# A fused block on Trainium2: differential attention that normalises and adds each unit as it comes, and a modulated weight made beside the gate scan

## The chip, the cores and the metric

The kernel runs on one core of a Trainium2 chip. The metric is the device time of one execution in microseconds (us). The engines are TensorE (PE for its matmuls, PEld for its weight loads), VectorE (DVE), ScalarE (ACT), GpSimd (POOL) and SyncE (SP), which issues DMAs. Each runs its own queue of instructions in order; they wait for each other through semaphores (`wait_ge`, `then_inc`).

## The reference, cut to what matters

The reference is a chain of eight stages over x of 8 batches x 256 tokens x 128 features, with a condition vector per batch. The change touches the last four; the first four (two attentions, a GRU-like scan with a top-1 mixture of experts, its routing) stay as they are.

```
# 1. gate scan: a recurrence over the 256 tokens, per batch, started from cond
g    = sigmoid(W_s s + W_x x_t + b)
s    = tanh(g * x_t + (1 - alpha) * s)
# 2. differential attention on the scan's states
q1,q2 = s @ w_q12 ; k1,k2 = s @ w_k12 ; v = s @ w_v
A    = softmax(q1 k1^T * scale) - lambda * softmax(q2 k2^T * scale)
o    = (1 - 0.8) * rmsnorm(A v)            # over the 128 features, eps 1e-5
x    = x + o
# 3. modulated linear map, per batch b
m    = (x * y_b) @ W / sqrt(sum((W*y_b)^2) + 1e-8)      # y_b = cond_b / sqrt(128)
# 4. top-2 mixture of 8 experts on m (silu gated, 512 wide), gate scores m @ gate^T
out  = x + sum over the two experts of p_e * expert_e(m)
```

(The listing is shortened by hand to the computation that the kernel carries out; q and k are 128 wide, 2,048 tokens in all.)

## The kernel before

`program` calls one function per stage; each opens a block in which every engine gets its list of instructions, and the engines meet between blocks. Features lie on the 128 partitions in `xT`, with the column of token t of batch b at 8 t + b.

**`gate_scan`** (block at L1555) runs 256 steps. In a step TensorE multiplies the state with `wT` (L1595), ScalarE takes the sigmoid (L1635), VectorE scans `targ` (L1676), ScalarE takes tanh (L1638) and VectorE scales the state by `leak` (L1673). TensorE fills the wait with 14 matmuls nobody reads (L1625). Work for later stages is dealt over the steps: every tenth step turns an expert weight (L1607, kept by ScalarE at L1645), and `plan` puts "qk" items (one matmul group, L1616) and "v" items (two strided blocks of states as stationary operands, L1621) on other steps, each with 4 fillers in place of 14 and copied by ScalarE one step later (L1656). `plan` avoids the steps of the weights.

**`diff_attention`** (block at L1723) first makes lambda (L1738, L1806), the modulation's sum (L1741), the last 32 tokens of q and k (L1749, copied at L1814) and the second half of the values (L1753, copied at L1817). Then 16 units, u = 2 b + half, each 128 queries against 256 keys of batch b. For unit u TensorE makes two score maps (`scores`, L1762), VectorE their maxima (`maxima`, L1874, L1876), ScalarE two exponentials with sums (`exps`, L1825), VectorE the reciprocals and the difference (`difference`, L1881 to L1889), TensorE turns it (`turn`, L1771), ScalarE keeps it (L1833), TensorE multiplies with the values (`attend`, L1780), VectorE copies the head (L1894) and ScalarE sums its squares (L1844). The orders are written out by hand: TensorE goes scores(u+2), attend(u-1), turn(u); VectorE maxima(u+1), difference(u), keep(u-1); ScalarE exps(u+1), keep(u), square(u-1). Two buffers each. After all units come one Sqrt (L1851), a reciprocal (L1905), 16 scalings (L1910), 16 transposes (L1800) and four additions into `xT` (L1915).

**`sparse_experts`** (block at L1991) first scales xT by `ys` (L2153), multiplies with `wmod` (L2009), scales by `dr` into `mB` (L2160), makes the gate scores (L2013) and copies them (L2178). Then the router: `best` twice (L2167 to L2175), counting, positions, lists. Beside it TensorE and ScalarE turn m and x to token-major `mt` and `xt` (L2004, L2089) and SP stores m to DRAM (`mrow`, L2334). POOL gathers blocks of 128 rows of `mrow` (L2312) once the lists are there, and 39 blocks go through the experts (L2049, L2058, L2066), are scattered to `yrow` (L2317), read back and added to `xt` (L2290).

Of the kernel before, what the change touches and what calls it, by code (L numbers as in the profile page):

```python
# [33 lines left out]
P = 128  # L34
# [27 lines left out]
def allocate(nc, ctx):  # L62
# [22 lines left out]
    n.ys, n.dr = sb("ys", [P, B]), sb("dr", [P, B])  # L85
# [6 lines left out]
    n.load_experts = ctx.enter_context(nc.semaphore("load_experts"))  # L92
    n.load_linear = ctx.enter_context(nc.semaphore("load_linear"))
# [1406 lines left out]
def gate_scan(nc, n, a, s2, qk, vt, wgT, wuT, wdT):  # L1500
# [13 lines left out]
    SPAN = 32  # L1514


    plan, at = {}, 0
    for p in range(T // SPAN - 1):
        at = max(at, SPAN * (p + 1))
        for item in [("qk", p, k) for k in range(4)] + ([("v", p, k) for k in range(4)] if SPAN * (p + 1) == P else []):  # L1520
            at += 1
            while (at - 4) % EVERY in (0, 1) or at % G == INPUTS_AT:
                at += 1
            plan[at] = (len(plan),) + item
    assert at < T
    with ExitStack() as local:
# [7 lines left out]
        leak = sb("leak", [P, 1])  # L1534
        ones_w = sb("ones_w", [1, B * G])
# [14 lines left out]
        arg_done = sem("s_arg"); state = sem("s_state")  # L1550

# [3 lines left out]
        with nc.Block() as block:  # L1555
# [12 lines left out]
            def _(pool):  # L1568
                for q in range(4):
                    w = TOK // 4  # L1570
                    out = pairs[:, 2 * w * q:2 * w * (q + 1)].rearrange("p (x two) -> p two x", two=2)[:, 0]
                    pool.tensor_copy(out, n.xT[:, w * q:w * q + w]).then_inc(z_in, 1)

            @block.tensor
            def _(pe):
# [16 lines left out]
                for s in range(T):  # L1592
# [16 lines left out]
                    if s in plan:  # L1609
# [3 lines left out]
                        if kind == "qk":  # L1613
# [3 lines left out]
                                                  s2[:, c0:c0 + B * SPAN], start=True, stop=True)  # L1617
                        else:
# [9 lines left out]
            def _(act):  # L1628
# [4 lines left out]
                for s in range(T):  # L1633
# [12 lines left out]
                    if s - 1 in plan:  # L1646
# [3 lines left out]
                        if kind == "qk":  # L1650
# [5 lines left out]
                        nc.scalar.activation(out, src, ACT.Copy).then_inc(pj_kept, 1)  # L1656
# [23 lines left out]
def diff_attention(nc, n, s2, qk, vt):  # L1680

    SPAN = 32
    MOD_EPS = 1e-8
# [3 lines left out]
    UNITS = B * SEG  # L1690
    with ExitStack() as local:
# [3 lines left out]
        def ps(name, shape):  # L1695
            return local.enter_context(nc.psum_tensor(name, shape, F32))
# [5 lines left out]
        negmax = [sb(f"negmax{i}", [P, 2]) for i in range(2)]  # L1702
        sums = [sb(f"sums{i}", [P, 2]) for i in range(2)]
        inv = [sb(f"inv{i}", [P, 2]) for i in range(2)]
# [3 lines left out]
        heads = sb("heads", [P, UNITS, D])  # L1708
        junk = sb("d_junk", [P, D])
        squares = sb("squares", [P, UNITS])  # L1710
        ys2, w2, dsum, mod_eps = sb("ys2", [P, B]), sb("w2", [P, D]), sb("dsum", [P, B]), sb("m_eps", [P, 1])
# [11 lines left out]
        with nc.Block() as block:  # L1723
# [10 lines left out]
            def _(pe):  # L1734
# [53 lines left out]
                for u in range(UNITS + 1):  # L1788
                    if u + 2 < UNITS:
                        scores(u + 2)  # L1790
                    if u >= 1:
                        attend(u - 1)
# [607 lines left out]
```

## Time and profile before

| what | value |
|---|---|
| runs before: median, lowest, highest | 1583.0, 1581.71, 1587.13 us |
| profiled execution: its time | 1581.07 us |
| its span, first to last instruction | 1579.0 us |
| TensorE matmul, VectorE, ScalarE, POOL busy | 93%, 46%, 41%, 7% of the span |
| mean granted TensorE clock | 0.946 of full (2.4 GHz) |

The span is what the trace covers; the execution's time has some 2 us around it. Busy shares are means over stages with different limits, and much of TensorE's share is filler, so the stages have to be read one by one. A line of a timeline gives the start in us from the span's start, the duration, the engine, the line of the kernel, the operation, output and input tiles, their shapes and how many instructions were merged. In brackets stands the idle time before it and who ended it.

### The profile page before, as it was taken

What the parts mean: (1) busy time and instruction counts of PE and PEld (TensorE: products, weight loads), DVE (VectorE), ACT (ScalarE), POOL (GpSimd) and SP (SyncE); (2) the same over time, 40 slices, a digit from 0 to 9 for tenths busy, and PEclk for the clock granted to TensorE, in tenths of its full rate; (3) what the DMA queues carried; (4) which work ended last, traced back from release to release, by engine and by line L of the source; (5) the groups of instructions that cost most, each with busy time, mean ns of one, the idle gap of its engine ahead of it and who ended that gap; (6) DMA issues with size and microseconds to landing.
All of it is one profiled execution on the core that took longest, in us unless ns stands there. A gap on an engine that the chain in (4) does not pass through costs nothing. (4 is left out here: it accounts for less than half of the span.)

```text
span 1579.0 us, 30235 instructions
## 1 busy us (share of the span) xinstructions
PE 1460.8 (93%) x11078; PEld 1132.5 (72%) x11078; DVE 732.8 (46%) x2721; ACT 651.0 (41%) x2429; POOL 106.7 (7%) x141
## 2 busy tenths in 40 slices
PE   7999978999989999999999998799999999767995
PEld 5333324777779999999999996488888888644663
DVE  3576765455433444444444445633333332863223
ACT  2322204565524554554554552134444443622442
POOL 4000000000000000000000000100000000004662
PEclk8999989999999999999999998599999999957998
DMA  5000000000030000000000000100000000001113
GB/s 158 1 0 0 1 0 1 1 1 1 1 108 1 1 2 2 1 2 1 2 1 2 1 2 1 34 21 22 22 22 28 22 2 1 1 27 33 42 43 96
DMA packets 27724, 27.95 MB, mean 18 GB/s; under 512 B 2293, under 2 KB 22234, under 8 KB 27450
## 3 DMA queue, kind: packets, MB, share of 16 engines
q1 hardware_dynamic: 20970, 16.70, 3.6%
q0 software_dynamic: 2496, 5.12, 1.1%
q10 hardware_dynamic: 4112, 4.19, 0.9%
q8 instruction: 90, 1.47, 0.4%
q14 instruction: 56, 0.46, 0.1%
HBM read 21.35 MB, written 4.65 MB: 16 GB/s over the span
## 5 line engine op out<-in xcount | busy, mean ns | idle before, releaser
L1625 PE MATMUL spare<-identb 128*128 128x128 bf16 x3166 | 218.4, 219 | 0.0
L1625 PEld LDWEIGHTS spare<-identb 128*128 128x128 bf16 x3166 | 202.0, 103 | 4.3
L1223 DVE TENSOR_TENSOR_SCAN narg<-rz,pre_n 128x16 f32<-128x16 f32 x256 | 47.9, 187 | 220.2 <-PE pre_n L1120 219.0
L1158 ACT ACTIVATE ghid<-gh_ps,cols 128x128 f32<-128x128 f32 x512 | 144.3, 365 | 12.9 <-PE gh_ps L1059 12.7
L1059 PE MATMUL gh_ps<-hist,w 128*128 128x128 f32 x1024 | 137.5, 275 | 0.6 <-ACT ghid L1158 0.6
L1068 PE MATMUL gy_ps<-w2e,ghid 128*128 128x128 f32 x1024 | 136.8, 276 | 0.8 <-DVE g_diff L1204 0.3
L1068 PEld LDWEIGHTS gy_ps<-w2e,ghid 128*128 128x128 f32 x1024 | 124.4, 191 | 3.2 <-issue 3.2
L1059 PEld LDWEIGHTS gh_ps<-hist,w 128*128 128x128 f32 x1024 | 125.9, 188 | 0.8 <-DVE hist L1231 0.8
L1144 ACT ACTIVATE rz<-pre_r 128x8 f32<-128x8 f32 x256 | 45.6, 178 | 181.9 <-PE pre_r L1120 179.2
L1120 PE MATMUL pre_r<-hist,gru_w 128*128 128x128 f32 x512 | 118.1, 311 | 0.8 <-DVE hist L1231 0.5
L1676 DVE TENSOR_TENSOR_SCAN targ<-gates,pairs 128x16 f32<-128x16 f32 x256 | 49.1, 192 | 140.8 <-ACT gates L1635 140.8
L1595 PEld LDWEIGHTS s_pre<-s,wT 128*128 128x128 f32 x512 | 77.0, 190 | 40.6 <-ACT s L1638 40.0
L1120 PE MATMUL pre_z<-hist,gru_w 128*128 128x128 f32 x512 | 99.9, 276 | 0.0
L1595 PE MATMUL s_pre<-s,wT 128*128 128x8 f32 x512 | 98.0, 264 | 2.0 <-ACT s L1638 0.4
L1120 PE MATMUL pre_n<-hist,gru_w 128*128 128x128 f32 x512 | 99.7, 276 | 0.0
L1673 DVE TENSOR_SCALAR pairs<-s,leak 128x8 f32<-128x8 f32 x256 | 59.6, 233 | 70.6 <-ACT s L1638 70.5
L1635 ACT ACTIVATE gates<-s_pre 128x8 f32<-128x8 f32 x256 | 45.5, 178 | 108.1 <-PE s_pre L1595 108.1
L634 DVE TENSOR_TENSOR term<-bc,kb 128x512 f32<-128x512 f32 x96 | 64.9, 686 | 53.3 <-PE bc L382 53.2
L1120 PEld LDWEIGHTS pre_r<-hist,gru_w 128*128 128x128 f32 x512 | 77.1, 190 | 16.0 <-DVE hist L1231 1.3
L1638 ACT ACTIVATE s<-targ 128x8 f32<-128x8 f32 x256 | 53.4, 209 | 83.9 <-DVE targ L1676 83.9
L1120 PEld LDWEIGHTS pre_n<-hist,gru_w 128*128 128x128 f32 x512 | 77.6, 189 | 0.0
L1120 PEld LDWEIGHTS pre_z<-hist,gru_w 128*128 128x128 f32 x512 | 77.5, 189 | 0.0
(412 smaller groups left out, 2516.4 us busy)
## 6 DMA issues: line engine op xcount, KB each, us to landing
w<-in_L_ffn_W SPq DMA_DIRECT2D x1, 2048.0 KB, 9.6
raw<-in_L_ffn_wg SPq DMA_DIRECT2D x8, 256.0 KB, 3.0
raw<-in_L_ffn_wu SPq DMA_DIRECT2D x8, 256.0 KB, 2.8
raw<-in_L_ffn_wd SPq DMA_DIRECT2D x8, 256.0 KB, 2.7
wqkv<-in_L_attn_Wqkv SPq DMA_DIRECT2D x1, 1536.0 KB, 6.6
mrow<-mt SPq DMA_DIRECT2D x4, 256.0 KB, 2.4
y_top<-yrow SPq DMA_DIRECT2D x4, 256.0 KB, 5.4
y_next<-yrow ACTq DMA_DIRECT2D x4, 256.0 KB, 5.8
```

The lines of the kernel that those rows point to most:

```text
L634: nc.vector.tensor_tensor(term[u % 2][:, j, :].rearrange("p (b t) -> p b t", b=GB), bc[k % 2][:, :].rearrange("p (b t) -> p b t", b=GB), k ...
L1059: mm = nc.tensor.matmul(h_ps[:, f, :], w1[:, e, P * f:P * f + P], tokens(g), start=True, stop=True)
L1068: mm = nc.tensor.matmul(y_ps, hid[v % 2][:, f, :], w2[:, e, f, :], start=(f == 0), stop=(f == NF - 1))
L1120: nc.tensor.matmul(out, n.gru_w[:, i, :], h, start=False, stop=True, skip_group_check=True).then_inc(ready, 1)
L1144: nc.scalar.activation(second(rz[s % 2][:, 0:16]), gate_slot(pre_r, s), ACT.Sigmoid).then_inc(r_done, 1)
L1158: nc.scalar.activation(hid[v % 2][:, f, :], h_ps[:, f, :], ACT.Relu, bias=n.cols[:, at:at + 1]).then_inc(h_done, 1)
L1223: V.tensor_tensor_scan(narg[p][:, :], rz[p][:, 0:16], n_slot(s), 0.0, ALU.mult, ALU.add).then_inc(narg_done, 1)
L1595: nc.tensor.matmul(pre[s // G % 2][:, at:at + B], wT[:, 0, :], s2[:, 8 * s:8 * s + B], start=False, stop=True, skip_group_check=True).then ...
L1625: nc.tensor.matmul(spare[:, 0:P], n.identb[:, :], n.identb[:, :], start=True, stop=True)
L1638: nc.scalar.activation(s2[:, 8 * s + 8:8 * s + 16], second(targ[s % 2][:, :]), ACT.Tanh).then_inc(state, 1)
L1673: nc.vector.tensor_scalar(second(pair), s2[:, 8 * s:8 * s + 8], leak[:, 0:1], None, ALU.mult).then_inc(leaked, 1)
L1676: nc.vector.tensor_tensor_scan(targ[s % 2][:, :], gates[s % 2][:, :], pair, 0.0, ALU.mult, ALU.add).then_inc(arg_done, 1)
```

## The change

The diff does five things.

1. `diff_attention` normalises each unit by itself. GpSimd computes `unit = (squares + least)^(-1/2)`, where `least` carries the epsilon and is scaled by the square of the first softmax's sum, since the difference is no longer divided by it: `difference` makes `ratio = sum0 * lambda / sum1` and one pass `probs1 * ratio + probs0`. ScalarE squares straight from PSUM with scale 1/GAIN.
2. The residual is token-major: `norm` adds `o * unit` into `xt[:, u, :]`. `xt` is filled in the gate scan by 8 "x" items (two transposes of strided columns of `xT` each).
3. Per batch a modulated weight `wb[:, b, :]` (128 columns of `W` scaled, then 8 gate columns) is made in the gate scan: one "mod" item, GpSimd's power and eight scalings (`wrow`), and 8 "w" items. In `diff_attention`, after the two norms of a batch, `turn_x(b)` transposes the new x, `keep_x(b)` copies it, `modulate(b)` multiplies with `wb`, `keep_m(b)` copies m and the gate scores into `mt`, and SP stores m per batch.
4. q is stored negated and scaled, so that VectorE takes minima and no scaling follows. The entry is reordered: q and k first, lambda behind them, values inside the units (`values(0)` behind `scores(0)`, `values(1)` to `values(3)` at the end of iterations 3, 7 and 11). ScalarE's Exp table is loaded ahead.
5. The front of `sparse_experts` up to the copy of the scores, and all its turning of m and x, are gone; it begins with `best` on `mt`.

```diff
 # gate_scan
+    put(4, [("x", 0, b) for b in range(B)])
+    put(20, [("mod", 0, 0)])
+    for p in range(T // SPAN - 1):
+        put(SPAN * (p + 1), [("qk", p, k) for k in range(4)])
+        if p == 0:
+            put(at, [("w", 0, b) for b in range(B)])
...
+                    if q == 0:
+                        pool.memset(power[:, :], -0.5).then_inc(mod_ready, 1)
+                        pool.tensor_scalar(ys[:, :], n.condT, float(D) ** -0.5, None, ALU.mult).then_inc(mod_ready, 1)
+                        pool.tensor_tensor(w2[:, :], n.wmod[:, :], n.wmod[:, :], ALU.mult).then_inc(mod_ready, 1)
+                        pool.wait_ge(mod_ready, 3)
+                        pool.tensor_tensor(ys2[:, :], ys[:, :], ys[:, :], ALU.mult).then_inc(mod_ready, 1)
+                pool.wait_ge(pj_kept, mod_item + 1)
+                pool.tensor_scalar(dr[:, :], modT[:, D:D + B], MOD_EPS, None, ALU.add).then_inc(dr_done, 1)
+                pool.wait_ge(dr_done, 1)
+                pool.tensor_tensor(dr[:, :], dr[:, :], power[:, :], ALU.pow).then_inc(dr_done, 1)
+                pool.wait_ge(dr_done, 2)
+                for b in range(B):
+                    pool.tensor_scalar(wrow[:, b, :], modT[:, 0:D], dr[:, b:b + 1], None, ALU.mult).then_inc(wrow_done, 1)
...
+                        elif kind == "x":
+                            for j in range(2):
+                                tokens = n.xT[:, :].rearrange("p (t b) -> p b t", b=B)[:, k, P * j:P * j + P]
+                                mm = nc.tensor.transpose(pj[i % 2][:, P * j:P * j + P], tokens, n.ident[:, :])
+                        elif kind == "mod":
+                            pe.wait_ge(mod_ready, 4)
+                            nc.tensor.transpose(pj[i % 2][:, 0:D], n.wmod[:, :], n.ident[:, :])
+                            mm = nc.tensor.matmul(pj[i % 2][:, D:D + B], w2[:, :], ys2[:, :], start=True, stop=True)
+                        elif kind == "w":
+                            pe.wait_ge(wrow_done, k + 1)
+                            g0 = ROWS["gate"][0]
+                            nc.tensor.transpose(pj[i % 2][:, 0:D], wrow[:, k, :], n.ident[:, :])
+                            mm = nc.tensor.matmul(pj[i % 2][:, D:D + E], wrow[:, k, :], n.cols[:, g0:g0 + E], start=True, stop=True)
 # diff_attention, GpSimd
+                for u in range(UNITS):
+                    one = slice(u, u + 1)
+                    pool.wait_ge(exp_done, 2 * u + 1)
+                    pool.tensor_scalar(least[:, one], sums[:, u, 0:1], D * EPS / GAIN ** 2, None, ALU.mult).then_inc(least_done, 1)
+                    pool.wait_ge(least_done, 2 * u + 1)
+                    pool.tensor_tensor(least[:, one], least[:, one], sums[:, u, 0:1], ALU.mult).then_inc(least_done, 1)
+                    pool.wait_ge(least_done, 2 * u + 2)
+                    pool.wait_ge(sq_done, u + 1)
+                    pool.tensor_tensor(mean[:, one], squares[:, one], least[:, one], ALU.add).then_inc(mean_done, 1)
+                    pool.wait_ge(mean_done, u + 1)
+                    pool.tensor_tensor(unit[:, one], mean[:, one], power[:, :], ALU.pow).then_inc(unit_done, 1)
 # TensorE
+                def turn_x(b):
+                    pe.wait_ge(normed, 2 * b + 2)
+                    pe.wait_ge(x_kept, turns["x", b])
+                    for i in range(SEG):
+                        mm = nc.tensor.transpose(x_ps[:, P * i:P * i + P], xt[:, SEG * b + i, :], n.ident[:, :])
+                    mm.then_inc(x_in, 1)
+
+                def modulate(b):
+                    pe.wait_ge(x_kept, turns["x", b] + 1)
+                    if b:
+                        pe.wait_ge(m_kept, b)
+                    for i in range(SEG):
+                        mm = nc.tensor.matmul(m_ps[:, M * i:M * i + M], xf[b % 2][:, i, :], wb[:, b, :], start=True, stop=True)
+                    mm.then_inc(m_in, 1)
...
+                for u in range(LAST + 1):
                     if u + 2 < UNITS:
                         scores(u + 2)
+                    if u >= 5 and u % 2:
+                        modulate((u - 5) // 2)
+                    if 1 <= u <= UNITS:
                         attend(u - 1)
                     if u < UNITS:
                         turn(u)
+                    if u in (3, 7, 11):
+                        values((u + 1) // 4)
+                    if u >= 4 and u % 2 == 0:
+                        turn_x((u - 4) // 2)
 # VectorE
+                    V.reciprocal(inv1[p][:, :], sums[:, u, 1:2]).then_inc(inv_done, 1)
...
+                    V.scalar_tensor_tensor(ratio[p][:, :], sums[:, u, 0:1], lam[:, 0:1], inv1[p][:, :],
+                                           ALU.mult, ALU.mult).then_inc(ratio_done, 1)
...
+                    V.scalar_tensor_tensor(diff[p][:, :], probs[p][:, 1, :], ratio[p][:, 0:1], probs[p][:, 0, :],
                                            ALU.mult, ALU.add).then_inc(diff_done, 1)
...
+                def norm(u):
+                    dve.wait_ge(unit_done, u + 1)
+                    V.scalar_tensor_tensor(xt[:, u, :], o_ps[u % 2], unit[:, u:u + 1], xt[:, u, :],
+                                           ALU.mult, ALU.add).then_inc(normed, 1)
...
+                minima(0)
+                keep_values(0)
+                for u in range(LAST + 1):
                     if u + 1 < UNITS:
+                        minima(u + 1)
+                    if u < UNITS:
+                        difference(u)
+                    if 2 <= u < UNITS + 2:
+                        norm(u - 2)
+                    if u in (3, 7, 11):
+                        keep_values((u + 1) // 4)
+                    if u >= 4 and u % 2 == 0:
+                        keep_x((u - 4) // 2)
+                    if u >= 5 and u % 2:
+                        keep_m((u - 5) // 2)
+            @block.sync
+            def _(sp):
+                for b in range(B):
+                    sp.wait_ge(m_kept, b + 1)
+                    sp.dma_start(mrow[T * b:T * b + T, :].rearrange("(i p) d -> p i d", p=P),
+                                 mt[:, SEG * b:SEG * b + SEG, 0:D]).then_inc(n.m_stored, 16)
 # sparse_experts, POOL
-                pool.wait_ge(m_stored, 16 * 4)
+                pool.wait_ge(n.m_stored, 16 * B)
```

## Rows read from the trace of the kernel before

**Rows 1.** Table of stretches: busy us and instructions per engine, clock, DMA
```profile
1332.70:1344.70 12.00, 10.38 (x35) 8.80 (x36) 0.68 (x5) 5.09 (x11) 0.99 (x4) 0.73 0.00 0
1344.70:1381.50 36.80, 28.25 (x150) 22.28 (x150) 32.40 (x110) 24.69 (x107) 0.00 (x0) 0.95 0.00 1
1381.50:1408.40 26.90, 18.04 (x67) 12.63 (x66) 15.04 (x34) 2.86 (x8) 1.81 (x10) 0.58 0.00 1
```

**Rows 2.** Timeline of the gate scan: a step with v, then one with qk
```profile
1185.32 1.19 PE L1621 MATMUL s_pj<-wv,s 128*128 128x128 f32 x4
...
1187.22 0.19 DVE L1676 TENSOR_TENSOR_SCAN targ<-gates,pairs 128x16 f32<-128x16 f32 x1 [0.75 <-ACT gates L1635]
...
1256.42 0.19 DVE L1676 TENSOR_TENSOR_SCAN targ<-gates,pairs 128x16 f32<-128x16 f32 x1 [0.49 <-ACT gates L1635]
...
1257.61 0.19 DVE L1676 TENSOR_TENSOR_SCAN targ<-gates,pairs 128x16 f32<-128x16 f32 x1 [0.49 <-ACT gates L1635]
```

**Rows 3.** Timeline of the attention's entry
```profile
1332.94 1.28 ACT L1806 ACT_TABLE_LOAD   x1 [0.31 <-PEq L1555]
...
1334.38 1.60 PE L1749 MATMUL dpj<-s,wq 128*128 128x256 f32 x4
...
1336.01 1.05 ACT L1814 ACTIVATE qk<-dpj 128x256 f32<-128x256 f32 x2 [1.28 <-PE dpj L1749]
...
1342.54 3.78 PE L1762 MATMUL s_ps<-qk 128*128 128x256 f32 x8 [0.47 <-ACT vt L1817]
1344.72 0.69 DVE L1874 TENSOR_REDUCE negmax<-s_ps 128x2 f32<-128x512 f32 x1 [9.93 <-PE s_ps L1762]
```

**Rows 4.** Timeline of one unit in the middle
```profile
1350.94 0.68 DVE L1874 TENSOR_REDUCE negmax<-s_ps 128x2 f32<-128x512 f32 x1
...
1351.74 0.16 DVE L1881 RECIPROCAL inv<-sums 128x2 f32<-128x2 f32 x1
...
1352.20 0.35 DVE L1887 TENSOR_SCALAR diff<-probs,inv 128x256 f32<-128x256 f32 x1
...
1352.59 0.48 DVE L1889 SCALAR_TENSOR_TENSOR diff<-probs,inv,diff 128x256 f32<-128x256 f32 x1
...
1352.99 0.28 DVE L1894 COPY heads<-o_ps 128x128 f32<-128x128 f32 x1
...
1353.13 0.44 PE L1771 MATMUL dt_ps<-ident,diff 128*128 128x128 f32 x2 [0.50 <-DVE diff L1889]
1353.19 0.68 DVE L1874 TENSOR_REDUCE negmax<-s_ps 128x2 f32<-128x512 f32 x1
...
1353.60 0.38 ACT L1833 ACTIVATE diffT<-dt_ps 128x256 f32<-128x256 f32 x1 [0.66 <-PE dt_ps L1771]
1353.88 0.30 ACT L1844 ACTIVATE d_junk<-heads 128x128 f32<-128x128 f32 x1
```

**Rows 5.** Timeline from the last difference to the router's first reduction
```profile
1380.96 0.48 DVE L1889 SCALAR_TENSOR_TENSOR diff<-probs,inv,diff 128x256 f32<-128x256 f32 x1
...
1382.41 1.04 PE L1780 MATMUL o_ps<-vt,diffT 128*128 128x128 f32 x4 [0.47 <-ACT diffT L1833]
...
1394.02 2.59 DVE L2153 TENSOR_TENSOR xs<-xT,ys 128x512 f32<-128x512 f32 x4 [0.32 <-PEq L1723]
...
1408.42 0.29 DVE L2167 TENSOR_REDUCE m_v<-m_val 128x16 f32<-128x128 f32 x1
```

**Rows 6.** POOL's groups by shape (busy us, mean ns), and one issue of SP
```profile
L260 POOL TENSOR_SCALAR_AFFINE_SELECT pick<-pick 96x1024 bf16<-96x1024 bf16 x9 | 11.7, 1305 | 1.3
L1731 POOL TENSOR_TENSOR ys<-ys 128x8 f32<-128x8 f32 x1 | 0.2, 202 | 0.0
...
1183.34 0.34 SPq L1565 DMA_DIRECT2D raw<-in_L_ffn_wd  x1
```

**Rows 7.** First expert matmuls, and the stretch before the clock came back
```profile
1433.78 2.07 PE L2049 MATMUL gu<-wgT,xgT 128*128 x2 [0.49 <-DVE xgT L2271]
...
1403.20:1437.20 34.00, 19.69 (x96) 14.97 (x96) 19.61 (x54) 9.41 (x13) 6.59 (x7) 0.50 0.16 43
```

More of the change, by code:

```diff
@@ L1514, in gate_scan, with put @@
     SPAN = 32
+    SCALE = float(D) ** -0.25
+    MOD_EPS = 1e-8
     plan, at = {}, 0
-    for p in range(T // SPAN - 1):
-        at = max(at, SPAN * (p + 1))
-        for item in [("qk", p, k) for k in range(4)] + ([("v", p, k) for k in range(4)] if SPAN * (p + 1) == P else []):
+    def put(earliest, items):
+        nonlocal at
+        at = max(at, earliest)
+        for item in items:
             at += 1
@@ L1550, in gate_scan @@
         arg_done = sem("s_arg"); state = sem("s_state")
+        mod_ready = sem("mod_ready"); dr_done = sem("dr_done"); wrow_done = sem("wrow_done")
+        mod_item = next(item[0] for item in plan.values() if item[1] == "mod")
         def second(ap):
@@ L1707, in diff_attention @@
         diffT = [sb(f"diffT{i}", [P, SEG, P]) for i in range(2)]
[L1708 to L1711, printed above, removed]
-        rms = sb("rms", [P, UNITS]); unit = sb("unit", [P, UNITS]); eps = sb("d_eps", [P, 1])
-        pj = [ps(f"dpj{i}", [P, 512]) for i in range(2)]
-        s_ps = [ps(f"s_ps{i}", [P, 2, T]) for i in range(2)]
@@ L1721, in diff_attention @@
-        rms_done = sem("d_rms"); mod_ready = sem("mod_ready"); mod_in = sem("mod_in"); mod_kept = sem("mod_kept"); unit_done = sem("d_unit"); normed = sem("d_normed"); back_in = sem("d_back"); added = sem("d_added")
+        junk = [sb(f"d_junk{i}", [P, D]) for i in range(2)]
+        squares, least, mean = sb("squares", [P, UNITS]), sb("least", [P, UNITS]), sb("d_mean", [P, UNITS])
+        power, unit = sb("d_power", [P, 1]), sb("unit", [P, UNITS])
+        xf = [sb(f"xf{i}", [P, SEG, P]) for i in range(2)]
@@ L1723, in diff_attention @@
+        turns = {key: i for i, (key, _) in enumerate(sorted(turns.items(), key=lambda kv: kv[1]))}
         with nc.Block() as block:
@@ L1896, in _ @@
-                maxima(0)
-                for u in range(UNITS):
-                    if u + 1 < UNITS:
-                        maxima(u + 1)
-                    difference(u)
-                    if u >= 1:
-                        keep(u - 1)
-                keep(UNITS - 1)
-                dve.wait_ge(rms_done, 1)
-                V.reciprocal(unit[:, :], rms[:, :]).then_inc(link, 1)
-                dve.wait_ge(mod_kept, 2)
-                V.reciprocal(n.dr[:, :], dsum[:, :])
-                dve.wait_ge(link, UNITS + 1)
@@ L2020, in _ @@
                 nc.tensor.matmul(cum_ps, tri[:, :], taken[:, :, :], start=True, stop=True).then_inc(counted, 1)
-                for g in range(4, 8):
-                    turn_tokens(g)
                 pe.wait_ge(pay_done, 2)
@@ L2095, in _ @@
                 act.preload_act_table(ACT.Silu)
-                for g in range(4, 8):
-                    keep_tokens(g)
                 act.wait_ge(const, 2)
```

290 lines of the change are left out of this document (122 added, 168 removed).

## The prediction, made before the changed kernel was seen

> **What bounds the kernel now.** I read the table of stretches first [rows 1]. The change touches four places: the gate scan (1011.5 to 1332.7 us), the entry of the differential attention up to the first `maxima` (12.0 us), its sixteen units (36.8 us), and what lies between the last unit and the router's first reduction (26.9 us). In the entry VectorE is busy for 0.7 us of 12; in the units it is busy 32.4 us of 36.8, more than TensorE (28.3) and ScalarE (24.7); in the last stretch no engine is full and TensorE is granted 0.58 of its clock. So entry and tail are chains of waits, and the units are bound by VectorE.
>
> The timeline of the scan [rows 2] shows that a step lasts 1.19 us from one `targ` to the next, also in a step with a "qk" item (1256.42 to 1257.61), but in one with a "v" item, whose four loads of strided states hold TensorE 1.19 us, VectorE waits 0.75 us for the gates and not 0.49: the step is 0.26 longer. In the entry [rows 3] TensorE does lambda, the modulation sum, four matmuls for q and k and eight for values; `scores(0)` starts at 1342.54 and VectorE's first reduction at 1344.72. In one unit [rows 4] VectorE's starts follow each other without a gap; reduction to reduction is 2.25 us, and the last difference starts at 1380.96 [rows 5], so it is the sixteenth after 36.2 us. In the tail [rows 5] the last heads are squared, a Sqrt table is loaded, sixteen scalings, sixteen transposes, four additions into xT, the scaling by ys, four wide matmuls and 32 small ones at the low clock follow each other, until the router reduces at 1408.42. From there to the end of the span are 170.6 us that the diff leaves in order.
>
> **Gate scan.** Added: 17 items (8 "x", 1 "mod", 8 "w"), none on the steps that turn expert weights. An x item loads two strided blocks and w loads three that are not strided, where the v item loads four strided ones; beside them ten fillers fall away, as in a qk item. An x item should hold TensorE about half of the v item's 1.19 us, and ScalarE's copies are no wider than qk's. The cover is the filler time of the step; without it each item costs up to 0.26, as v does: 17 x 0.26 = 4.4 us. POOL's work (a sum of small operations and eight 128x128 scalings) runs beside about four steps. I take +0.3 us for all this; bounds 0 and 4.4. POOL's first power is also here, twelve steps before a w item wants it, so a slow first one is covered.
>
> **Entry.** Removed from the path: the wait for lambda and the modulation sum ahead of q and k, and the values, of which `values(0)` now stands behind `scores(0)` and the others inside the units. TensorE can start at about 1332.95. ScalarE loads its table until 1334.22 and copies q and k in four parts, 1.05 us for two [rows 3]: done at 1334.24 + 2.1 = 1336.35. q's four matmuls took 1.60 us where the stretch's clock was 0.73, so both are ready by 1336.2 at that rate and near 1334.6 at twice it. Then `scores(0)`: before, 2.18 us passed from its start to the reduction, at the low clock; at the full one half of it. First reduction: 1336.4 + 1.6 = 1338.0 (bounds 1337.3 and 1339.5) against 1344.72, a gain of 6.7 us (5.2 to 7.4). Lambda's exponential now comes behind the copies, at 1336.5, and is in time.
>
> **The units.** From VectorE's unit go the scaling of the maximum, one wide pass (`tensor_scalar` over 256) and the copy of the head; in come the norm (like the copy, 0.20 to the next start), and per unit from the fifth on one of `keep_x` and `keep_m` (a copy of 256 or 272 columns, about 0.35 to the next start from the 128-column copy's 0.20). Let d be the start of the difference's last pass. From the reduction's start to it: 0.62 (reduction to an independent follower; 0.80 less the scaling) + 0.46 (reciprocal to the pass after next [rows 4]) = about 1.05. Behind it 0.40 to the norm and 0.20 to what follows. Without keeps a step is 1.65, with one 2.0, against 2.25. But `keep_x(b)` waits for `turn_x(b)`, which stands in TensorE's order behind `turn(u)`, and this for this very difference: turn starts at d + 0.53 and ends at d + 0.98 [rows 4], two more transposes end at d + 1.22, so the copy starts at d + 1.26 instead of d + 0.62. VectorE, the bound engine, stalls 0.64 us in each even unit, and behind the waiting copy stand the next reduction and with it ScalarE's next exponentials: step 2.64. The odd ones are 2.01, because `modulate(b)` ran ahead of turn. The mean is 2.33, slightly over 2.25. In units 3, 7 and 11 `keep_values` waits for four strided loads behind turn (1.0 us more than the turn): d + 2.0, so steps of 3.4, 3.75 and 3.75.
> A second chain floors the step. The unit's turn (d + 0.98), ScalarE's copy (0.28 to the next start) and square with its accumulator (0.4), then POOL's addition and power, and the norm comes at the next d + 0.40: step at least 1.3 + 0.3 of waits + power = 1.6 + x. POOL's nearest row is 0.20 us for 128x8 [rows 6]; the dearest compute row with a repeated cost is 1.3 us (96x1024). I take x = 0.3, nearest the small tile; bounds 0.1 and 1.3.
> Steps between the sixteen differences: 1.45, 1.45, 2.05, 3.4, then (2.64, 2.01, 2.64, 3.75) twice, 2.64, 2.01, and 2.02 (no reduction in the last): 37.1. The first difference comes 2.95 after the first reduction, since `values(0)` pushes `scores(1)` back 1.0 us. 40.1 against 36.2: +3.8, and +0.7 for the first scores at the low clock: +4.5 us (bounds +2 and +6, without the power).
>
> The Trainium skill (SBUF — State Buffer, section Who interferes with whom) says that a VectorE instruction with two SBUF inputs and a GpSimd instruction that reads SBUF exclude each other for their whole length; the difference's last pass (0.48 us) is such a one. No row of the trace shows POOL and VectorE together in this stage. By the rule POOL's pair would be pushed behind that pass in the even units only, where the norm's delay of some 0.4 us hides in the wait for `turn_x`; the sum would change by two or three of the early steps, +1 us.
>
> **Tail.** From the end of the last difference (E = 1381.44) the new chain is: turn E + 0.49, ScalarE's copy 0.90, attend 1.6 (1.04 at the fallen clock [rows 5]), square 2.1, POOL 2.1 to 2.65, norm 2.95, turn_x 3.6, keep_x 4.0, modulate 4.9, keep_m 5.3, SP's issue of the last store 0.34 [rows 6], the change of block 0.32 [rows 5], the small ramp 0.25: E + 6.2 (bounds 5.6 and 7.5). Before: 1408.42 - 1381.44 = 27.0. Gain 20.8 us. The store itself is far ahead of the gathers, which wait for the lists 20 us later.
> Behind it the order is the same. But the first expert matmuls already ran at half clock for 3.5 us (1433.78 to 1437.2 [rows 7]), and TensorE now does less ahead of them: +0.8 us, between 0 (as now) and 2.
>
> **Sum.** +0.3 - 6.7 + 4.5 - 20.8 + 0.8 = -21.9. The profiled execution took 1581.07 us, its span and 2.1 around it: 1559.2. The median of the runs is 1.9 above it, so against that 1561.1; I forecast 1560.0.
>
> **Rivals.**
> The power is dear but bounded (1.3 us as POOL's large row): all steps under 2.9 grow to 2.9, 14 steps sum to 7.2 more, and the tail 1.0: 1568. For it: no row shows a power, and it should be no cheaper than an addition; against: it is one column, not 1,024.
> The other side: POOL's chain becomes the bound. From x = 2.4 us the fourteen steps of 1.6 + x (and x in the tail) eat all 21.9 us; at 3.0 us the time is 1591. For it: the trace has no row of its kind; against: 2.4 us is twelve times POOL's small tile [rows 6].
> The items in the scan don't fit: each costs as v does: 1564.
> The turns don't stall VectorE (its own steps 1.65 and 2.0, the values hidden): twelve steps of 2.0, four of some 1.7 and a first one of 2.0, 33 us instead of 40: 1553. Against: the order written for TensorE puts each turn behind `turn(u)`.
>
> **Chances.** The forecast 0.62 (its own range 1556 to 1566); dear power 0.15; slow items 0.10; no stalls 0.09; POOL the bound 0.04. Range of 8 in 10: 1552 to 1570. This kernel's measurement can't tell under 0.3% (4.7 us): only POOL's bound, or one near it, ends there: faster 0.94, same 0.03, slower 0.03.
>
> **What would show it.** Reductions that start near 1338; difference starts apart by 2.6 and 2.0 in turn with `xf` copies waiting for TensorE in the even units; scan steps of 1.19 with x and w items; the power's row at 0.3; some 6 us from the last difference to the router's first reduction. A POOL row of microseconds for the power, or `norm` waiting in every unit, would make it wrong.

## The result, and the profile of the changed kernel

The changed kernel took 1563.9 us (median of 4 runs, 1560.8 to 1565.1) beside 1582.4 us for the kernel before (4 runs, 1575.4 to 1587.1); the ratio of the runs is 0.989, with a 95% interval from 0.986 to 0.993. The forecast was 1560.0 us in a range of 1552 to 1570. The profiled executions span 1579.0 and 1563.3 us, 15.7 us apart. Of a kernel further down (E6) one execution of four took 3400.8 us, which nothing on record explains; it is left out of that kernel's ratio.

The two traces, cut at the same instructions (a stretch runs from the start of one to the start of the next):

| stretch, us | before | after | change | predicted |
|---|---|---|---|---|
| start to the first `targ` (no line on its way changed) | 1017.30 | 1019.54 | +2.24 | 0 |
| gate scan, to the last `targ` | 314.90 | 317.60 | +2.70 | +0.3 |
| entry, to the first reduction | 12.52 | 5.23 | -7.29 | -6.7 |
| units, to the start of the last difference | 36.24 | 41.20 | +4.96 | +4.5 |
| tail, to the router's first reduction | 27.46 | 8.53 | -18.93 | -20.8 |
| router, to the first `gu` weight load | 25.25 | 25.35 | +0.10 | 0 |
| experts, to the end | 145.33 | 145.89 | +0.56 | +0.8 |

The first line is no effect of the change: over twelve profiled executions, one of each kernel in this document and all with the same stages up to there, that stretch took between 1015.6 and 1023.2 us, so the time of a single profile can't settle 5 us. It is left out from here on. Behind it the change took away 17.9 us. A stretch in which the clock does the same can be read to tenths; the scan and the tail can't, where the clock falls at another place, and the scan of the eight kernels that have it as changed took 316.5 to 320.6 us.

The table of stretches, in the columns of [rows 1]: scan, entry, units, tail, and the stretch in which the clock is low.

```profile
1019.50:1337.10 317.60, 310.54 (x3736) 264.70 (x3735) 108.43 (x510) 130.82 (x607) 6.62 (x10) 0.98 0.06 18
1337.14:1342.37 5.23, 4.02 (x27) 3.51 (x25) 0.87 (x5) 3.40 (x7) 0.10 (x1) 1.00 0.00 0
1342.37:1383.57 41.20, 33.86 (x197) 28.55 (x197) 31.54 (x91) 25.45 (x107) 16.02 (x56) 1.00 0.06 17
1383.58:1392.10 8.52, 4.54 (x25) 3.16 (x24) 3.62 (x10) 1.01 (x5) 3.07 (x10) 0.78 0.11 35
1388.30:1422.40 34.10, 10.73 (x48) 5.84 (x49) 21.22 (x58) 3.46 (x4) 9.32 (x18) 0.50 0.08 22
```

In the units VectorE is busy for less than before (31.5 us, [rows 1] 32.4) and yet they take 5 us more: the engine waits. The granted clock of TensorE is 1.00 in entry and units, and 0.98 in the scan, where before nothing was missing.

In the scan, a step with an x item and then the place where a step was long:

```profile
1033.70 0.49 PE L1652 MATMUL s_pj<-ident,xT 128*128 128x128 f32 x2
...
1034.13 0.19 DVE L1729 TENSOR_TENSOR_SCAN targ<-gates,pairs 128x16 f32<-128x16 f32 x1 [0.49 <-ACT gates L1679]
...
1074.51 0.19 DVE L1729 TENSOR_TENSOR_SCAN targ<-gates,pairs 128x16 f32<-128x16 f32 x1 [0.49 <-ACT gates L1679]
...
1074.74 1.70 PE L1669 MATMUL spare<-identb 128*128 128x128 bf16 x14
...
1077.09 0.19 DVE L1729 TENSOR_TENSOR_SCAN targ<-gates,pairs 128x16 f32<-128x16 f32 x1 [1.88 <-ACT gates L1679]
```

The x item holds TensorE for 0.49 us, under half of the v item's 1.19 [rows 2], and its step waits 0.49 as a qk step does. The later step, in which TensorE also turns an expert weight, is 2.58 us long; the same step took 1.45 us before. It holds none of the new items: its fourteen filler matmuls take 1.70 us. From 1074.3 to 1077.7, and again from 1084.5 to 1087.9, the granted clock is half (1.2 GHz of 2.4):

```profile
1074.30:1077.70 3.40, 3.40 (x31) 3.34 (x30) 0.76 (x4) 1.15 (x6) 0.00 (x0) 0.50 0.27 77
```

The entry, in the columns of [rows 3]:

```profile
1337.93 1.10 PE L1807 MATMUL dx_ps<-s,wq 128*128 128x256 f32 x4 [0.30 <-PEq L1573]
...
1339.18 1.05 ACT L1897 ACTIVATE qk<-dx_ps 128x256 f32<-128x256 f32 x2
...
1341.14 1.13 PE L1832 MATMUL s_ps<-qk 128*128 128x256 f32 x4 [0.91 <-ACT qk L1897]
...
1342.38 0.69 DVE L1952 TENSOR_REDUCE floor<-s_ps 128x2 f32<-128x512 f32 x1 [0.89 <-PE s_ps L1832]
```

A pair of units, in the columns of [rows 4]: the even one with `turn_x` and `keep_x`, then the odd one.

```profile
1354.12 0.48 DVE L1966 SCALAR_TENSOR_TENSOR diff<-probs,ratio 128x256 f32<-128x256 f32 x1
...
1354.52 0.35 DVE L1971 SCALAR_TENSOR_TENSOR xt<-o_ps,unit,xt 128x128 f32<-128x128 f32 x1
...
1354.66 0.44 PE L1841 MATMUL dt_ps<-ident,diff 128*128 128x128 f32 x2 [0.72 <-DVE diff L1966]
...
1354.94 0.38 PE L1861 MATMUL dx_ps<-ident,xt 128*128 128x128 f32 x2
...
1355.36 0.42 DVE L1983 COPY xf<-dx_ps 128x256 f32<-128x256 f32 x1 [0.49 <-PE dx_ps L1861]
...
1356.81 0.49 DVE L1966 SCALAR_TENSOR_TENSOR diff<-probs,ratio 128x256 f32<-128x256 f32 x1
...
1356.84 0.22 POOL L1793 TENSOR_SCALAR least<-d_sums 128x1 f32<-128x1 f32 x1
```

VectorE ends the norm at 1354.87 and then waits 0.49 us for TensorE's `dx_ps`, which stands behind the turn of the same difference: difference to difference 2.69 us. In the whole attention its waits, in us, times and longest, are:

```profile
DVE vt L1977 <- PE dx_ps L1824: 3.7, 3, 1.2
DVE xt L1971 <- POOL unit L1800: 3.0, 3, 1.4
...
DVE xf L1983 <- PE dx_ps L1861: 2.8, 7, 0.5
```

GpSimd's group of the power in the units, in the columns of [rows 6], with it the one power of the gate scan (eight columns) and the additions that are its neighbours:

```profile
L1800 POOL TENSOR_TENSOR unit<-d_mean,d_power 128x1 f32<-128x1 f32 x16 | 9.1, 568 | 1.3
...
L1798 POOL TENSOR_TENSOR d_mean<-squares,least 128x1 f32<-128x1 f32 x16 | 3.1, 191 | 21.2 <-ACT d_junk L1922 21.1
...
L1600 POOL TENSOR_TENSOR dr<-dr,s_power 128x8 f32<-128x8 f32 x1 | 1.7, 1693 | 0.1
```

One power of 128x1 takes 568 ns where an addition of the same shape takes 191. With eight columns a power takes 1693 ns, where a multiplication took 202 [rows 6]: if the price grows evenly between the two shapes, each further column costs some 160 ns (an estimate from these two rows). The tail, in the columns of [rows 5]:

```profile
1385.67 0.57 POOL L1800 TENSOR_TENSOR unit<-d_mean,d_power 128x1 f32<-128x1 f32 x1
...
1385.98 0.19 ACT L1922 ACTIVATION_READ_ACCUMULATOR d_junk<-o_ps 128x1 f32 x1
...
1386.32 0.22 POOL L1793 TENSOR_SCALAR least<-d_sums 128x1 f32<-128x1 f32 x1
...
1387.16 0.57 POOL L1800 TENSOR_TENSOR unit<-d_mean,d_power 128x1 f32<-128x1 f32 x1
1387.77 0.35 DVE L1971 SCALAR_TENSOR_TENSOR xt<-o_ps,unit,xt 128x128 f32<-128x128 f32 x1 [0.81 <-POOL unit L1800]
...
1389.30 1.27 PE L1869 MATMUL dm_ps<-wb,xf 128*128 128x136 f32 x4 [0.52 <-DVE xf L1983]
1390.61 0.44 DVE L1987 COPY mt<-dm_ps 128x272 f32<-128x272 f32 x1 [1.36 <-PE dm_ps L1869]
...
1391.88 0.19 DVE L2205 TENSOR_SCALAR m_iota<-iota 128x8 f32<-128x8 f32 x1 [0.83 <-PEq L1785]
1392.11 0.29 DVE L2212 TENSOR_REDUCE m_v<-mt 128x16 f32<-128x128 f32 x1
```

The last unit's squares are ready at 1386.17, but GpSimd is still in unit 14's power until 1386.24 and has then this unit's two `least` products to do; the last power ends at 1387.73. From 1388.3 the clock is half, so `modulate` takes 1.27 us where the same line takes 0.73 some 2 us earlier.

### The profile page after: what moved, and what is told of

Read it like the earlier page. It is cut to its first block and busy times, and to the rows that moved or that the text cites. A ratio compares the mean times of both kernels' runs of the same rounds, so it can differ in the third digit from the quotient of the medians.

```text
span 1563.3 us, 29989 instructions
## 1 busy us (share of the span) xinstructions
PE 1440.9 (92%) x10908; PEld 1119.0 (72%) x10909; DVE 720.6 (46%) x2677; ACT 646.6 (41%) x2429; POOL 132.0 (8%) x216
## 5 line engine op out<-in xcount | busy, mean ns | idle before, releaser
L1669 PE MATMUL spare<-identb 128*128 128x128 bf16 x2996 | 211.5, 221 | 0.0
L1669 PEld LDWEIGHTS spare<-identb 128*128 128x128 bf16 x2996 | 195.0, 104 | 4.5
```

What stands on the lines that cost most here:

```text
L1669: nc.tensor.matmul(spare[:, 0:P], n.identb[:, :], n.identb[:, :], start=True, stop=True)
```

## The experiments

Ten kernels were run, each an edit of the changed kernel. Their stretches from one profile each, in us; kernels that were sent together ran beside the kernel before on one chip, which took 1585.7 us beside the first four, 1577.7 beside E5 to E8 and 1580.1 beside the last two.

| kernel | scan | entry | units | tail | router | experts | time |
|---|---|---|---|---|---|---|---|
| changed | 317.60 | 5.23 | 41.20 | 8.53 | 25.35 | 145.89 | 1565.1 |
| E1 power as addition | 316.50 | 5.23 | 40.77 | 9.83 | 25.36 | 146.18 | 1563.0 |
| E2 turn_x first | 320.64 | 5.23 | 38.15 | 8.63 | 25.34 | 145.63 | 1567.6 |
| E3 values and turn_x first | 317.65 | 5.23 | 35.79 | 7.84 | 25.29 | 145.46 | 1556.2 |
| E4 fillers in w | 315.10 | 5.23 | 41.20 | 7.81 | 25.19 | 146.32 | 1562.2 |
| E5 floors ahead | 316.54 | 5.23 | 41.21 | 7.30 | 25.27 | 145.46 | 1566.0 |
| E6 combined | 314.83 | 5.24 | 35.80 | 7.42 | 25.30 | 144.94 | 1551.8 |
| E7 combined, busy router | 314.83 | 5.23 | 35.78 | 7.42 | 25.24 | 145.02 | 1550.9 |
| E8 power twice | 317.68 | 5.23 | 42.04 | 9.73 | 25.27 | 145.03 | 1564.1 |
| E9 values in entry | 317.66 | 5.23 | 42.42 | 8.69 | 25.36 | 145.33 | 1565.9 |
| E10 power four times | 317.69 | 5.24 | 48.27 | 12.90 | 25.26 | 145.34 | 1574.5 |

Times are those of the profiled executions. Router and experts are cut at the first `gu` weight load.

### E1: the power as an addition

```diff
-pool.tensor_tensor(unit[:, one], mean[:, one], power[:, :], ALU.pow)
+pool.tensor_tensor(unit[:, one], mean[:, one], power[:, :], ALU.add)
```

> The changed kernel with GpSimd's power in the units replaced by an addition of the same tiles (the norm is left out of the computation, its instruction and its waits stay). In the changed kernel the power's row is 0.57 us and an addition's 0.19. Stage read: from the first reduction to the last difference 41.2 us, from there to the router's first reduction 8.5 us. Theory (VectorE's own passes and its waits for TensorE's turns set the steps, GpSimd's chain only where no copy stands in a unit and at the end): only the steps that wait for unit get shorter, 0.4 to 1.2 us in the units, and 0.4 to 0.8 in the tail. Rival (GpSimd's chain sets the steps): 0.38 in each of 14 steps, 5 us in the units.

GpSimd's last instruction of a unit went from 568 to 191 ns, 6 us over 16 units. The units became 0.43 us shorter, and 0.39 of that is one step, the third, where the norm of unit 0 waits for the first power (2.60 to 2.21 us). All steps from the fourth on stayed. So in the loop the power's price is hidden beside other work, but for the third step. The tail can't be read as its price: there the clock fell ahead of the last difference, 40.3 us after the first reduction and not 45.9.

### E2 and E3: TensorE's order in the units

E2 puts `turn_x` ahead of `turn(u)`; E3 puts the values, too, ahead of `attend` and `turn`:

```diff
+if u in (3, 7, 11): values((u + 1) // 4)
 if 1 <= u <= UNITS: attend(u - 1)
+if u >= 4 and u % 2 == 0: turn_x((u - 4) // 2)
 if u < UNITS: turn(u)
-if u in (3, 7, 11): values((u + 1) // 4)
-if u >= 4 and u % 2 == 0: turn_x((u - 4) // 2)
```

> In TensorE's order turn_x(b) stands ahead of turn(u), its inputs being ready one iteration earlier. Theory (VectorE stalls at keep_x because turn_x is queued behind the turn that waits for this very difference): the even steps fall from 2.69 to between 2.13 (VectorE's own passes) and 2.25 (GpSimd's chain with a power of 0.57), five steps, so 2.2 to 2.8 us less in the 41.2 us of the units; the steps of 3.41 and 3.77 stay. Rival (the even step is set by TensorE's or ScalarE's work, not by the order): the steps stay at 2.69.

> As the one before, and values(k) stand right behind the scores of iterations 3, 7 and 11 and not behind the turn. Theory: the steps of 3.41, 3.77 and 3.77 fall to what VectorE's own passes need, 2.1, 2.5 and 2.5, or some 0.5 more where TensorE (scores 0.9, values 1.0, modulate 0.5, attend 0.5, turn 0.4 in one iteration, 3.3 us) becomes the bound: 2.3 to 3.8 us less than with turn_x alone. Rival (the copy of the values waits for the strided loads wherever they stand): no less than with turn_x alone.

With E2 the units took 3.05 us less: the even steps fell from 2.69 to 2.11 us, the odd ones rose from 2.13 to 2.28, the last fell from 2.10 to 1.51. That is a little more than the 2.2 to 2.8 us that were expected: the five even steps gave 2.9, the last one 0.6, and the odd ones took 0.5 back. With E3 they took 5.41 us less than in the changed kernel; the step with values in unit 3 fell from 3.41 to 2.10, those in 7 and 11 from 3.77 to 2.82 and 2.87. The same work is done, in another order. VectorE's waits for the turned rows (`xf`) are gone, and those for the values (`vt`) fell from 3.7 to 0.5 us. The first even step, the one shown, still takes 2.65 us:

```profile
1350.46 0.48 DVE L1966 SCALAR_TENSOR_TENSOR diff<-probs,ratio 128x256 f32<-128x256 f32 x1
...
1350.63 0.74 POOL L1800 TENSOR_TENSOR unit<-d_mean,d_power 128x1 f32<-128x1 f32 x1
...
1350.68 0.38 PE L1861 MATMUL dx_ps<-ident,xt 128*128 128x128 f32 x2
...
1351.00 0.44 PE L1841 MATMUL dt_ps<-ident,diff 128*128 128x128 f32 x2
...
1351.40 0.35 DVE L1971 SCALAR_TENSOR_TENSOR xt<-o_ps,unit,xt 128x128 f32<-128x128 f32 x1 [0.46 <-POOL unit L1800]
...
1351.67 0.41 DVE L1983 COPY xf<-dx_ps 128x256 f32<-128x256 f32 x1
```

`keep_x` starts at once behind the norm. (What is left, in this unit, is the norm's own wait for GpSimd, whose power takes 0.74 us here; in the whole attention it comes to 3.6 us in 5 units.) E2 as a whole was no gain, since its scan took 320.6 us: the clock fell there in the x items, which the edit doesn't touch, for 10.3 us from 13.3 us after the first `targ`, and twice more later.

### E4: eight fillers behind the items of the modulated weight

```diff
-fill = FILL // 3
+fill = 8 if kind == "w" else FILL // 3
```

> The changed kernel with 8 fillers in place of 4 behind each w item of the gate scan. In the changed kernel TensorE was granted half its clock for 3.4 us twice, from the sixth w item on and once more behind the eighth, and four steps took 2.6 us more than before; the scan took 317.6 us from the first targ to the last against 314.9. Theory (with the few columns of a w item and 4 fillers TensorE does too little to keep its clock): the clock stays, the scan takes 314.9 to 315.3 us. Rival 1 (the items themselves are in the way: ScalarE's copies, GpSimd beside VectorE): 317.6 as before. Rival 2 (8 fillers overrun the step): the clock stays, but each of the eight steps gets 0.1 to 0.2 us longer, 316 us.

The scan took 315.10 us, 2.5 less, and within 0.2 of before, as the theory had it and neither rival. In all eight kernels with four fillers behind the w items the clock fell there once or twice, in the three with eight (E4, E6, E7) it didn't. In the stretch of the w items the table of stretches says for this kernel

```profile
1070.00:1095.00 25.00, 24.73 (x310) 21.09 (x308) 8.62 (x41) 11.10 (x53) 0.00 (x0) 1.00 0.08 23
```

and for the changed kernel

```profile
1070.00:1095.00 25.00, 23.44 (x248) 20.47 (x245) 7.64 (x36) 10.33 (x49) 0.00 (x0) 0.86 0.08 23
```

More matmuls that compute nothing, a clock of 1.00 in place of 0.86, and 41 VectorE instructions done in place of 36.

### E5: the floor of the next unit ahead of the wait for the squares

```diff
+floors(0)
 for u in range(UNITS):
+    floors(u + 1)      # the two products into least
-    ...                # the same two, for u
     pool.wait_ge(sq_done, u + 1)
```

> Both products of the floor of unit u+1 are issued on GpSimd before it waits for the squares of unit u, so the last unit's floor no longer stands behind unit 14's power. The theory that the units are bound by VectorE and TensorE expects the stretch from the first reduction to the last difference unchanged (41.2 us, within 0.3), and the last norm about 0.5 us earlier, so a tail of about 8.0 us in place of 8.53. The theory that GpSimd's chain costs time in the middle of the loop too expects 1 to 2 us off the units, since the wait behind the power there goes as well.

The units didn't move (41.21 us). The tail is 1.23 us shorter. The last power ends 3.56 us after the last difference's start and not 4.15, 0.6 sooner where 0.5 was expected; the rest of the 1.23 is the clock, which in this execution fell 1.1 us later, so that the last modulation ran at full speed.

### E8 and E10: the power two and four times

```diff
+for i in range(N):      # 1 in E8, 3 in E10
+    pool.tensor_tensor(again[:, i, one], mean[:, one], power[:, :], ALU.pow)
 pool.tensor_tensor(unit[:, one], mean[:, one], power[:, :], ALU.pow)
```

> GpSimd raises each unit's mean to the power twice, the first into a tile that nothing reads: 0.57 us more on GpSimd in each unit (0.62 with its issue). If GpSimd's chain has the margin that the trace shows (the norm waited for it in 3 of 16 units), the units grow by little, 0 to 1.5 us in the odd steps of 2.13 us, and the tail by 0.6 to 1.2 us: 1 to 2.5 us in all. If GpSimd's chain is what sets the pace, all 16 units pay 0.6 us, about 9 us more, 1572 us. Halfway between: GpSimd's work for a unit is then about 1.9 us with its waits, below the mean step of 2.6 us.

> GpSimd raises each unit's mean to the power four times, three of them into a tile that nothing reads: 2.27 us for the power, about 2.9 us for its busy work in a unit and some 3.1 us with its issues, over the mean step of 2.65 us. The theory that a second power cost nothing because GpSimd has room within a unit (two units stand between a difference and its norm) expects this one to be bound by GpSimd: 16 x 3.1 = 49 to 50 us for the units in place of 41.2, and the tail 2.5 to 3 us longer: about 1575 us. The rival, that the norm's wait is a matter of order alone, expects less than 3 us in the units.

A second power cost 0.84 us over the units (0.52 of it in the third step, 0.1 in each odd one) and 1.20 in the tail. Four of them made GpSimd the bound, 7.1 us more in the units and 4.4 in the tail; GpSimd's own timeline has the period:

```profile
1359.84 0.19 POOL L1798 TENSOR_TENSOR d_mean<-squares,least 128x1 f32<-128x1 f32 x1
...
1360.11 1.73 POOL L1801 TENSOR_TENSOR again<-d_mean,d_power 128x1 f32<-128x1 f32 x3
...
1361.81 0.55 POOL L1802 TENSOR_TENSOR unit<-d_mean,d_power 128x1 f32<-128x1 f32 x1
...
1362.44 0.22 POOL L1793 TENSOR_SCALAR least<-d_sums 128x1 f32<-128x1 f32 x1
...
1362.75 0.19 POOL L1795 TENSOR_TENSOR least<-least,d_sums 128x1 f32<-128x1 f32 x1
...
1363.02 0.19 POOL L1798 TENSOR_TENSOR d_mean<-squares,least 128x1 f32<-128x1 f32 x1
```

3.18 us from one `d_mean` to the next with no idle place, and VectorE's waits for the norm in this kernel:

```profile
DVE xt L1973 <- POOL unit L1802: 19.8, 16, 2.8
```

16 waits where the changed kernel has 3. I had expected 49 to 50 us for the units; they took 48.3, because the first steps, ahead of the first norm, don't pay. In the tail 2.5 to 3 us were expected: the last power ends 4.3 us later than in the changed kernel, since unit 14's four powers stand ahead of unit 15's.

### E9: the values in the entry again

```diff
 scores(0)
-values(0)
+for k in range(4): values(k)
 scores(1)
```

with `keep_values` beside it, and neither in the units.

> The values of all four pairs are turned and kept in the entry again, between the first two score products, and none inside the units. What the prediction priced: in the units the steps that now take 3.41 and 3.77 us fall to 2.1, so 1.3 + 2 x 1.65 = 4.6 us less; ahead of the first difference three more turns and copies, one behind the other on one bank, 3 x (0.9 to 1.4 us) = 2.7 to 4.2 us more. The first reduction doesn't move (entry 5.23). Together the stretch from the first reduction to the last difference is 0.4 to 1.9 us shorter, about 40 us. The rival: the four values are hidden in the early units anyway and the whole 4.6 us come back, 36.6 us.

The stretch grew by 1.22 us where a gain of 0.4 to 1.9 was expected. The steps gave back 4.9 us, priced at 4.6 (3.41 to 1.77, and twice 3.77 to 2.13), but the first difference came 8.84 us after the first reduction and not 2.69:

```profile
1343.16 0.42 DVE L1976 COPY vt<-dx_ps 128x256 f32<-128x256 f32 x1
...
1344.89 0.42 DVE L1976 COPY vt<-dx_ps 128x256 f32<-128x256 f32 x1 [1.31 <-PE dx_ps L1824]
```

Matmuls and copy take turns on one bank, 1.73 us a pair of heads, and `scores(1)` behind them ran in part at half clock (it fell for 3.4 us from 4.9 us after the first reduction), for 6.15 us in all. So the values inside the units, stalls and all, cost 1.2 us less than four in a row on one bank; how much of this the half clock added no run separates.

### E6 and E7: the edits together, and a busier router

E6 is E3 and E5 with eight fillers behind both w and x items. E7 adds to it 155 fillers in the router, 35 at its start, 80 ahead of the wait for `pay` and 40 ahead of the one for the owners.

> The three edits together: the values turned ahead of attend and turn, 8 filler matmuls in place of 4 behind the items of the modulated weight and of the token-major turn, and the floors a unit ahead. If they add up: scan about 315.0 us (317.6 in the changed kernel), units about 35.6 us (41.2), tail about 7.4 us (8.5), so about 9 us under the changed kernel, a time of about 1554 us. If the clock falls elsewhere instead (it fell once in the scan of nearly every run), the scan's 2.6 us don't come and the time is 1557 us.

> The combined kernel with 155 filler matmuls of TensorE (128 columns, bf16, into a bank that the router doesn't read) in three places of the router, while TensorE has little to do. If the half clock at the start of the experts is due to TensorE's idleness in the router and comes back with work, the stretch from the first expert matmul to the end is 2 to 2.5 us shorter (143.5 in place of 145.9) and the stretch of the router is unchanged: a time 2 us under the combined kernel's. The rival: the fillers stand ahead of TensorE's few small products of the router and delay them (the router's stretch 1 to 3 us longer), or the clock falls all the same, and the time is the same or longer.

E6 against the kernel before: ratio 0.986, 95% interval 0.983 to 0.989; E7: 0.987 (0.984 to 0.989). By stretches behind the first `targ` E6 takes 533.5 us, the changed kernel 543.8, before 561.7. All three edits came through: scan -2.8, units -5.4, tail -1.1, and another 0.9 in the experts. By the ratios of the runs E6 is only 5 to 6 us ahead of the changed kernel, and the two intervals overlap, so the 10 us rest on one profile of each.

The fillers of E7 brought nothing. They did bring the clock back, but only while they ran; around the first expert matmuls the table of stretches has

```profile
1400.30:1403.70 3.40, 1.30 (x14) 0.78 (x11) 0.43 (x2) 0.00 (x0) 2.49 (x4) 1.00 0.15 47
1403.72:1407.13 3.41, 2.97 (x4) 1.43 (x5) 0.14 (x1) 0.60 (x1) 2.50 (x4) 0.50 0.16 47
```

TensorE had 1.3 us of work in the 3.4 us ahead of the first expert matmul (1404.16), waiting for the gathered rows, and the clock fell 0.4 us before that matmul. It came back at 1407.1, 71.5 us after the first reduction, where in E6 it came back at 71.6. So E7 didn't reach what it was built to test: what the experts would take with a full clock from their first matmul on, no run shows.

## Why the prediction was right, step by step

**Entry, -7.3 us for -6.7: right.** The order of the steps was as written. Of the remaining 0.6 us 0.2 are ScalarE's four copies (1.9 us, where 2.1 were taken from [rows 3]) and 0.4 the clock: from the start of the first scores to the reduction 1.24 us passed at full speed, where the sum had 1.6.

**Units, +5.0 us for +4.5: the mechanism right, one term missing and one that did not come.** Steps forecast at 2.64, 2.01, 3.4 and 3.75 measured 2.69, 2.13, 3.41 and 3.77, and E2 and E3 show the cause, TensorE's order and not VectorE's work. The odd step's 0.12 is a copy of `mt` that takes 0.43 us in place of 0.35. The third step took 2.60 us, not 2.05, since it pays for the first power (E1: 2.21 without). Against that, "+0.7 for the first scores at the low clock" did not come. 3.8 and 0.7 made 4.5; measured the steps are 1.4 over their sum of 37.1, and the first difference 0.26 under its 2.95. So errors of either sign cancelled here. (The rival without stalls summed sixteen steps where there are fifteen; E3, in which nearly all of the turns' stalls are gone, took 35.8 us and not 33.)

**The power: the size wrong, and the bound built on it too.** I took 0.3 us of bounds 0.1 and 1.3; it is 0.57. The forecast survived because the "second chain" doesn't floor each step. The text had the norm at the *next* difference, "step at least 1.6 + x", which gives 2.74 us for E8 and 3.9 for E10, in every step. Measured were 2.69 and 2.22 in turn for E8, and for E10 3.2 on average from the fifth step to the fourteenth. The norm of a unit comes two differences later (VectorE's loop calls `norm(u - 2)` behind `difference(u)`), so the chain has two steps to run in, and what floors a step is GpSimd's own occupancy: the power and about 0.9 us for the rest, as E10's rows show. By that the rival in which GpSimd is the bound eats the gain later than at 2.4 us: with four powers, 2.3 us, the units of E10 took 48.3 us where steps of 3.9 would have made some 58. That this error did the forecast no harm is luck: the power was cheap enough for both readings of the chain to leave the steps alone.

**Tail, -18.9 us for -20.8: the mechanism right, the size 1.9 us off.** The sum had E + 6.2 us, with E the end of the last difference; measured are 8.05. The squares were ready at E + 2.1, as written. From there to the end of the power were 1.56 us and not 0.55: 0.27 for the dearer power, about 0.15 for the handovers on GpSimd, and 0.6 for the queue, which is unit 14's power (to 1386.24) and behind it the two `least` products (E5 takes 0.6 of it away). From the power to the end of the copy into `mt` it was 0.7 more, of which 0.4 are `modulate` at half clock; from there to the reduction 0.15 more (1.06 for the issue, the block change and the ramp, written as 0.91). What the prediction missed is GpSimd's in-order queue: I had listed its `least` products nowhere.

**Gate scan, +2.7 us for +0.3: wrong, for a reason not in the list.** The rival was that each item overruns its cover; the x and w items didn't (in their steps 1.19 us from one `targ` to the next). What was overlooked is that the cover, the fillers, is also what TensorE does: a w item has two small products and four fillers, and the clock fell twice there. The 14-filler steps behind took 2.58 us in place of 1.45 (with the turned weight), and 1.47, 1.71 and 1.84 in place of 1.19: 2.6 us together. E4 brought 2.5 us back with four fillers more in each w item. By chance it could have been more or less: 316.5 us in E1 and E5, where the clock fell once, 320.6 in E2.

**Experts, +0.6 us for +0.8: right.** The first expert matmuls ran at half clock for 4.9 us (before 3.5). Over the twelve profiles the two go together: 2.9 to 3.0 us at half clock and 144.9 to 145.0 us (E6, E7, E8), 3.4 to 3.7 and 145.3 (before, E9, E10), 3.9 to 4.4 and 145.5 to 145.6 (E5, E3, E2), 4.8 to 5.2 and 145.9 to 146.3 (the changed kernel, E4, E1), some 0.5 us for each us. That the shorter tail is why it is 4.9 is only argued; when the clock comes back relative to the first `gu` varies between these runs.

The errors: scan +2.4, tail +1.9, units +0.5, entry -0.6, experts -0.2 make 3.9 us, with the router's 0.1 4.0. No one of them is over 2.5 us of 22, so the total held; but only 0.8 us of them pull the other way, and with the clock falls of E2 in the scan the time would have been 3 us longer.

**GpSimd beside VectorE.** The forecast text weighed a rule and priced it at +1 us. The traces show it at work, but not as told. In the changed kernel one instruction of GpSimd is held for long:

```profile
1350.71 0.48 DVE L1966 SCALAR_TENSOR_TENSOR diff<-probs,ratio 128x256 f32<-128x256 f32 x1
...
1350.96 0.31 POOL L1793 TENSOR_SCALAR least<-d_sums 128x1 f32<-128x1 f32 x1
...
1358.88 0.57 POOL L1800 TENSOR_TENSOR unit<-d_mean,d_power 128x1 f32<-128x1 f32 x1
...
1358.94 0.48 DVE L1966 SCALAR_TENSOR_TENSOR diff<-probs,ratio 128x256 f32<-128x256 f32 x1
```

This `least` starts 0.26 us into the pass and takes 0.31 us in place of 0.22: it ends as if it had begun 0.34 us after the pass did. The power at 1350.63 in E3 starts 0.17 us into a pass and takes 0.74 us in place of 0.57, again as one begun 0.34 us behind the pass's start, and the norm of that unit waits 0.46 us for it. In all profiles of the changed kernel and the ten experiments every GpSimd instruction that starts between 0.06 and 0.34 us into such a pass is held to that same point; the shortest wait is 0.01 us and the longest 0.28. Two kinds are not held. Where GpSimd starts 0.03 to 0.06 us behind the pass, as at 1356.84, it takes its usual 0.22 us, and the pass takes 0.01 to 0.04 us longer (0.49 there). Where it starts first, as at 1358.88, both have their usual lengths. The Trainium skill (SBUF — State Buffer, section Who interferes with whom) has such a pair exclude each other; the traces agree for a GpSimd instruction that comes second by more than 0.06 us, and only for the first 0.34 us of a pass of 0.48, and they don't show it where GpSimd comes first: a 0.57 us power and a 0.48 us pass run together. The +1 us did not come: in the changed kernel the held times sum to some 0.15 us.

## What to carry to other kernels

Where an edit puts a new product on TensorE inside a loop, ask what it stands behind in the written order, and for what the next engine is then waiting: here the same work in another order was worth 5.4 us of 41. A side chain (GpSimd's) is priced twice: by the number of steps between the work that feeds it and its reader, and by its own occupancy, and at the end of the loop every instruction of its queue counts in full. Fillers that are taken out to make room for work have to be counted as TensorE's activity too.

## What the hardware showed unexpectedly

- A power of one column on GpSimd takes 568 ns, three additions' time (191), and one of eight columns 1693 ns, eight times a multiplication's 202.
- A GpSimd instruction that starts 0.06 to 0.34 us into VectorE's two-input pass of 0.48 us ends as if begun 0.34 us behind the pass's start; one that starts earlier than that, or ahead of the pass, isn't held.
- The clock fell in work that looks dense: at the w items TensorE was busy for 23.4 of 25 us by the records and the clock stood at 0.86 over the stretch; with 24.7 of 25 it stood at 1.00. In one of the nine profiles of kernels with four fillers behind the x items (E2's) it fell there too, for 10.3 us, and cost some 3 us.
- 155 filler matmuls in the router gave the clock back for as long as they ran; with 1.3 us of work in the 3.4 us behind them it fell again 0.4 us before the experts' first matmul.
